# Spreading a pass's last projections, moving a residual product into the attention block and its loads with it

## The chip, the cores and the metric

One core of a Trainium2 chip runs the kernel. TensorE multiplies matrices, VectorE, ScalarE and GpSimd work elementwise, SyncE issues the loads and stores. The engines run on their own and wait for each other by semaphores. The metric is the device time of one execution, in microseconds.

## The reference

One layer of a perceiver, in f32. `x` is 512 x 512, the context 8192 x 512.

```python
x = x + cross_attention(layernorm(x), ctx)      # 16 heads of 32; q, k, v and output with bias bq, bk, bv, bo
x = x + sparse_self_attention(layernorm(x))     # per-head layernorm of q and k with an affine; sparse mixing
x = x + mixture_of_experts(layernorm(x))        # 8 experts, 2 per row
```

The change touches the first line and the layer norm that the second begins with:

```python
k = ctx @ Wk.T + bk; v = ctx @ Wv.T + bv
a = softmax(q @ k.T * 32 ** -0.5) @ v
x = x + a @ Wo.T + bo
h = (x - mean(x)) / sqrt(var(x) + 1e-5)
```

## The kernel before

The layer runs as a row of blocks. At the end of a block all engines meet before the next begins. A tensor of 512 x 512 is held as [128, 4, 512].

**First pass** (`prepare`, then `project_context`). The context comes in 16 chunks of 512 rows. Each chunk gives four outputs of 128 x 512 for the keys and four for the values, 128 outputs in all (`ITEMS` holds their order; the last three items are values). An output is the sum of 12 matmuls of 512 columns: `split_product` adds three products of high and low parts for each of four slices. Beside them run 256 steps of scores: step i writes scores of key differences (`dif`, one PSUM bank pair) and key sums (`tot`, two pairs); ScalarE takes the absolute value of `dif` (line 451), VectorE adds it to `tot` and keeps the maximum (line 480). On TensorE step i is: `scores(i + 1, dif)`, which waits until ScalarE has read the last `dif`; `scores(i, tot)`; and six projection matmuls, half an output, in steps 0 to 245. The last ten steps have none. In `finished(i)` ScalarE evacuates an output that is ready (`evacuate`: line 439 for keys, 443 for values), VectorE makes the low part of keys (`low`), and SyncE stores both to DRAM (line 340 for values). The block ends when the stores have landed.

**Second pass** (`attend_context`). Four groups of four heads; in each, 64 tiles of 128 context rows (16 chunks of four tiles). Per tile: scores of four heads (line 631), exponentials (ScalarE, line 694, two of 1024 columns), the weighted values (line 645), and on VectorE a running sum of the exponentials over runs of nine or ten tiles (lines 729 to 731), which `sums` adds up on TensorE (line 661). SyncE loads keys and values of chunk m into one of three buffers when chunk m - 3 has been scored (lines 599, 604). Behind chunk 2 it issues the output weights `woT`, the four weight matrices of self attention and the affine rows (lines 606, 861, 863). The shift of the next group's softmax is turned on TensorE in tile 9, copied by VectorE to `stage` (line 750), and taken by GpSimd into the rows of `c.stacks` (`take_row`, line 568); the scores of the next group wait for that. When a group is done, the sums are inverted (line 738) and `weigh` makes `aoT` from them: on GpSimd for the first three groups, on VectorE for the last (lines 572, 574).

**Residual** (`add_and_normalise` named "xo", a block of its own). For each of four tiles TensorE multiplies a row of ones by `bo` (line 790) and adds four products of `aoT` with `woT` (line 792; a product in f32 shows as two records), VectorE adds the tile to `x` and makes mean and variance (lines 805 to 811), ScalarE the square root, VectorE the inverse and the normalised tile (lines 814, 816). TensorE then turns all tiles (line 798), ScalarE and VectorE copy them to `hT`. Meanwhile SyncE loads the mixing weights (`load_mixing`): one part at once, the rest in 16 loads (line 854) when the last residual tile is done, since they overwrite `aoT` and `woT`.

**Self attention's projections** (`self_projections`). TensorE begins with queries (line 913). VectorE first waits for all mixing weights and reduces them (lines 986 to 995), and then centres the queries (line 958).

## Time and profile before

| | us |
|---|---|
| median of 3 runs | 1740.19 |
| the runs | 1730.46, 1740.19, 1740.70 |
| the profiled execution | 1736.88 |
| its span, first to last instruction | 1735.2 |
| TensorE (PE) busy in it | 1554.2, 90% |
| VectorE (DVE) busy | 1191.6, 69% |
| ScalarE (ACT) busy | 967.6, 56% |
| GpSimd (POOL) busy | 355.7, 20% |

The profile has these views: busy time by windows, with the clock that TensorE was granted (1.00 is 2.4 GHz, 0.50 is 1.2 GHz) and the busy share of the DMA engines; the timeline, in which neighbouring instructions of one kind are merged into a row with their count; and one line's or tile's instructions. PE is a matmul and PEld a weight load, SPq is SyncE's queue of DMAs. The end of a matmul is modelled, so its duration holds some of the pipeline; the distance between starts tells the rate. Rows of GpSimd are rough.

The first pass runs from 50 to 578 us, the second from 578.75 to 1171, the residual's block from there to 1201.5, self attention and the experts to the end.

### The profile page before, as it was taken

The page shows a single profiled execution, that of the slowest core. Times are in us where ns is not written, and L with a number is a line of the kernel's source. Part 1 is how long each engine was busy: PE and PEld are TensorE (multiplying, and loading weights), DVE is VectorE, ACT ScalarE, POOL GpSimd, SP SyncE. Part 2 cuts the span into 40 slices and gives each one's busy share as a digit, 9 for nine tenths or more (in the row PEclk, how much of TensorE's full clock was granted, in tenths as well). Part 3 has the DMA queues.
Part 4 walks back from the last instruction along what each step waited for, and adds up shares of the span by engine and source line. Part 5 has one row for each costly group of instructions (what it writes and reads, how often), then busy time and mean ns, then how long its engine had stood idle before and what let it go on. Part 6 is the DMA issues. An engine that isn't in the chain of part 4 may idle for free. (4 is left out here: it accounts for less than half of the span.)

```text
span 1735.2 us, 21727 instructions
## 1 busy us (share of the span) xinstructions
PE 1554.2 (90%) x8000; PEld 820.5 (47%) x8000; DVE 1191.6 (69%) x1836; ACT 967.6 (56%) x1165; POOL 355.7 (20%) x138
## 2 busy tenths in 40 slices
PE   6799999999999699999999999988877506699998
PEld 4466666666665233333333333323343204577775
DVE  5677677677676789999999999993865493220002
ACT  2466666666666678888888888860444501011110
POOL 4463563563560110030021001001000000100001
PEclk9899999999999699999999999998968857799999
DMA  4445445445345664444444444414100280379993
GB/s 171 175 164 184 142 161 185 142 159 188 136 162 146 197 143 121 116 115 118 115 120 122 121 116 118 117 40 73 31 19 1 85 309 2 111 246 327 326 329 109
DMA packets 117194, 250.00 MB, mean 144 GB/s; under 512 B 9689, under 2 KB 26073, under 8 KB 112610
## 3 DMA queue, kind: packets, MB, share of 16 engines
q1 hardware_dynamic: 115376, 244.42, 45.2%
q0 software_dynamic: 1280, 4.20, 0.7%
q8 instruction: 64, 1.05, 0.3%
q14 instruction: 40, 0.33, 0.1%
q10 hardware_dynamic: 434, 0.01, 0.0%
HBM read 182.00 MB, written 61.34 MB: 140 GB/s over the span
## 5 line engine op out<-in xcount | busy, mean ns | idle before, releaser
L694 ACT ACTIVATE att_pr<-att_sc 128x1024 f32<-128x1024 f32 x512 | 496.3, 1022 | 79.7 <-PE att_sc L631 79.7
L731 DVE TENSOR_TENSOR att_tot<-att_tot,att_pr 128x2048 f32<-128x2048 f32 x200 | 463.6, 2318 | 26.0 <-ACT att_pr L694 5.8
L480 DVE CUSTOM_DVE_ANT_0 ctx_size<-ctx_tot,ctx_size 128x512 f32<-128x512 f32 x512 | 332.9, 688 | 143.9 <-PE ctx_tot L399 139.8
L451 ACT ACTIVATE ctx_size<-ctx_dif 128x1024 f32<-128x1024 f32 x256 | 262.3, 1025 | 127.6 <-PE ctx_dif L399 127.6
L631 PE MATMUL att_sc<-g_stacks,att_kst 98*128 98x512 f32 x1024 | 309.9, 425 | 4.9 <-DMA att_kst<-keys_scratch 3.3
L631 PEld LDWEIGHTS att_sc<-g_stacks,att_kst 98*128 98x128 f32 x1024 | 173.9, 189 | 241.4 <-ACT att_pr L694 212.3
L645 PE MATMUL att_o<-att_pr,att_val 128*32 128x512 f32 x2048 | 274.5, 608 | 1.3 <-issue 1.2
L399 PE MATMUL ctx_dif<-ctx_k_dif,f_q_hi 32*128 32x512 f32 x512 | 129.4, 503 | 17.3 <-ACT ctx_size L451 10.1
L1661 ACT ACTIVATE ex_hidT<-ex_hp,m_b 128x128 f32<-128x128 f32 x120 | 34.2, 367 | 196.0 <-PE ex_hp L1616 193.6
L399 PE MATMUL ctx_tot<-ctx_k_sum,f_q_hi 32*128 32x512 f32 x512 | 130.0, 506 | 0.0
L1616 PEld LDWEIGHTS ex_hp<-ex_xT,m_w 128*128 128x128 f32 x960 | 109.4, 192 | 8.0 <-issue 8.0
L1616 PE MATMUL ex_hp<-ex_xT,m_w 128*128 128x128 f32 x960 | 109.8, 275 | 0.8 <-issue 0.8
L1629 PE MATMUL ex_yp<-m_w,ex_hidT 128*128 128x512 f32 x240 | 105.5, 592 | 0.0
L399 PEld LDWEIGHTS ctx_dif<-ctx_k_dif,f_q_hi 32*128 32x128 f32 x512 | 48.1, 184 | 112.7 <-issue 54.8
L101 POOL TENSOR_TENSOR g_stacks<-f_raw,g_stacks 128x2048 fp32r<-128x2048 f32 x21 | 96.7, 4604 | 1.7
L572 POOL TENSOR_TENSOR o_aoT<-att_whole,att_rs 128x512 f32<-128x512 f32 x3 | 9.4, 3138 | 385.6 <-DVE att_rs L738 385.6
L645 PEld LDWEIGHTS att_o<-att_pr,att_val 128*32 128x32 f32 x2048 | 40.5, 108 | 96.5 <-issue 95.2
L85 PE MATMUL f_proj<-g_stacks,f_wk_hi 128*128 128x512 f32 x176 | 78.0, 443 | 0.5 <-DVE f_k_lo L208 0.5
L1669 DVE COPY ex_xT<-ex_tx 128x512 f32<-128x512 f32 x15 | 10.4, 692 | 94.9 <-PE ex_tx L1570 88.8
L731 DVE TENSOR_TENSOR att_tot<-att_pr 128x2048 f32<-128x2048 f32 x28 | 64.0, 2287 | 14.1 <-ACT att_pr L694 14.1
L1675 DVE COPY o_yT<-ex_yp 128x512 f32<-128x512 f32 x15 | 10.4, 691 | 91.4 <-PE ex_yp L1629 91.4
L85 PE MATMUL f_proj<-f_wv_hi,g_stacks 128*128 128x512 f32 x160 | 71.3, 445 | 0.0
(273 smaller groups left out, 2118.6 us busy)
## 6 DMA issues: line engine op xcount, KB each, us to landing
m_w<-in_W SPq DMA_DIRECT2D x30, 2048.0 KB, 13.5
att_kst<-keys_scratch SPq DMA_DIRECT2D x192, 256.0 KB, 4.0
f_raw<-in_ctx SPq DMA_DIRECT2D x32, 1024.0 KB, 6.0
keys_scratch<-f_k_hi SPq DMA_DIRECT2D x32, 512.0 KB, 2.8
keys_scratch<-f_k_lo SPq DMA_DIRECT2D x32, 512.0 KB, 3.2
values_scratch<-ctx_v SPq DMA_DIRECT2D x32, 512.0 KB, 3.3
att_val<-values_scratch SPq DMA_DIRECT2D x64, 256.0 KB, 2.7
rows_scratch<-mix_blank SPq DMA_DIRECT2D x1, 3840.0 KB, 26.5
```

Source lines behind the costliest of these rows:

```text
L85: pe.matmul(out, ah, bh, start=(first and i == 0), stop=False)
L101: pool.tensor_tensor(c.lo[b], raw[:, :, :], f32(c.hi[b]), ALU.subtract).then_inc(c.s_lo, 1)
L399: mm = pe.matmul(out[:, r * CH:(r + 1) * CH], c.q_hi[rows, g, t * P:(t + 1) * P], keys[m % 2][rows, g, :], start=True, stop=True)
L451: act.activation(size[:, i % ABS, :], dif[:, :], ACT.Abs).then_inc(s_size, 1)
L480: dve.tensor_tensor_reduce(out=size[:, i % ABS, r * CH:(r + 1) * CH], in0=tot[i % 2][:, r * CH:(r + 1) * CH], in1=size[:, i % ABS, r * CH: ...
L631: mm = pe.matmul(sc[pair % PAIRS][:, r * N:(r + 1) * N], kst[m % CHUNKS][:, j, at:at + P], c.stacks[0:STK + 2, HG * (T // PER_G) + j, :], ...
L645: mm = pe.matmul(o[at, :], val[m % CHUNKS][:, T % KT, at], pr[:, T % SLOTS, j, :], start=first, stop=False, skip_group_check=True)
L694: act.activation(pr[:, T % SLOTS, 2 * s:2 * s + 2, :], sc[(2 * T + s) % PAIRS][:, :].rearrange("p (j q) -> p j q", j=2), ACT.Exp, scale=SC ...
L731: dve.tensor_tensor(tot[b % 2][:, :, :], so_far, pr[:, T % SLOTS, :, :], ALU.add).then_inc(s_add, 1)
L1616: mm = pe.matmul(hp[tau % 2][:, f, :], w1[b][:, k, f * P:(f + 1) * P], xT[tau % 2][:, k, :], start=(k == 0), stop=(k == DC - 1))
L1629: mm = pe.matmul(yp[tau % 2][:, :], hidT[tau % 2][:, f, :], w2[b][:, f, :], start=(f == 0), stop=(f == FC - 1))
L1661: act.activation(hidT[tau % 2][:, f, :], hp[tau % 2][:, f, :], ACT.Relu, bias=b1[:, f, :]).then_inc(s_hid, 1)
```

## The change

`split_product` takes a range of the 12 matmuls of an output. The first 228 steps of the first pass have six of them as before, steps 228 to 254 have four. The block "xo" is gone. The bias comes broadcast over 128 partitions and is added to `x` by GpSimd early in the second pass. In the second pass's own block TensorE multiplies the three finished groups with the output weights, for tile 0 before the last sums and for tiles 1 to 3 after them, then adds the last group; VectorE normalises tile t - 1 after the moments of tile t, tiles are turned one by one, and ScalarE alone copies them. The affine rows are loaded after chunk 8, self attention's matrices after chunks 17, 19, 21 and 23, the output weights after chunk 32; the mixing weights are loaded in this block too. The core of the diff:

```diff
@@ project_context
-    LAST = 2 * (len(ITEMS) * KT - FIRST)
+    WHOLE = 3 * DC
+    WIDE, NARROW = WHOLE // 2, WHOLE // 3
+    CUT = (WHOLE * (len(ITEMS) * KT - FIRST) - NARROW * (STEPS - 1)) // (WIDE - NARROW)
+    def begun(i):
+        return WIDE * min(i, CUT) + NARROW * max(i - CUT, 0)
+    def pieces(i):
+        at, end = begun(i), min(begun(i + 1), WHOLE * (len(ITEMS) * KT - FIRST))
+        while at < end:
+            stop = min(end, at - at % WHOLE + WHOLE)
+            yield FIRST + at // WHOLE, at % WHOLE, at % WHOLE + stop - at
+            at = stop
     def finished(i):
-        return [FIRST + (i - 1) // 2] if i % 2 == 0 and 0 < i <= LAST else []
+        return [o for o, _, end in pieces(i - 1) if end == WHOLE] if i else []
...
                 scores(i, tot[i % 2], k_sum, s_tot)
-                if i < LAST:
-                    project(FIRST + i // 2, i % 2)
+                for piece in pieces(i):
+                    project(*piece)
@@ attend_context
+        xh = pr[:, (TILES - 2) % SLOTS - 2, :, :]
+        banks = [sc[(2 * TILES - n) % PAIRS][:, half * N:(half + 1) * N] for n in (3, 2, 1) for half in range(2)]
+        acc, tp = banks[0:NT], banks[NT:] + [o[:, :], den[:, :]]
@@ gpsimd, after the memsets
+            pool.wait_ge(s_ones, CHUNKS)
+            pool.wait_ge(bo_in, 16)
+            for t in range(NT):
+                pool.tensor_tensor(c.x[:, t, :], c.x[:, t, :], c.yT[:, 2, :], ALU.add).then_inc(s_bo, 1)
+            pool.wait_ge(s_bo, NT)
@@ sync, in the loop over chunks m
-                if m == CHUNKS - 1:
+                if m == NCH // 2:
+                    sp.dma_start(c.yT[:, 2, :], c.dram["bo"].broadcast_to([P, D])).then_inc(bo_in, 16)
+                    load_affine(sp, c)
+                if NCH <= m < NCH + 2 * len(SELF_WEIGHTS) and m % 2:
+                    load_self_weight(sp, c, m // 2 - NCH // 2)
+                if m == 2 * NCH:
                     sp.dma_start(c.woT[:, :, :], ...).then_inc(c.wo_in, 16)
-                    load_self_weights(sp, c)
+            sp.wait_ge(s_row[0], HG // 2 + HG * (G - 1))
+            sp.wait_ge(s_bo, NT)
+            load_mixing(sp, c, s_mm)
@@ tensor, after the last tile
+            pe.wait_ge(c.wo_in, 16)
+            pe.wait_ge(s_out, G - 1)
+            residual(0, range(G - 1))
             sums(len(starts) - 1)
+            for t in range(1, NT):
+                residual(t, range(G - 1))
+            pe.wait_ge(s_out, G)
+            for t in range(NT):
+                residual(t, [G - 1]).then_inc(s_mm, 1)
+            for t in range(NT):
+                pe.wait_ge(s_h, t + 1)
+                for k in range(DC):
+                    mm = pe.transpose(tp[t][:, k * P:(k + 1) * P], xh[:, t, k * P:(k + 1) * P], c.ident[:, :])
+                mm.then_inc(s_tp, 1)
@@ scalar, after the last exponential
+            for t in range(NT):
+                act.wait_ge(s_var, t + 1)
+                act.activation(std[:, t:t + 1], std[:, t:t + 1], ACT.Sqrt).then_inc(s_std, 1)
+                if t >= 1:
+                    turned_rows(t - 1)
+            turned_rows(NT - 1)
@@ vector, after weigh(dve, G - 1)
+            dve.wait_ge(s_bo, NT)
+            for t in range(NT):
+                moments(t)
+                if t >= 1:
+                    normalised(t - 1)
+            normalised(NT - 1)
@@ perceiver_layer
                 attend_context(nc, c)
-                add_and_normalise(nc, c, "xo", c.aoT, c.woT, c.wo_in, c.hT, bias=c.bo[:, :],
-                                  meanwhile=load_mixing)
```

`residual(t, groups)` multiplies `aoT` with `woT` for those groups into `acc[t]`; `moments(t)` is the addition, the two statistics and the epsilon of the old block, `normalised(t)` its inverse and product; `turned_rows(t)` copies one turned tile.

## Rows read from the trace of the kernel before

**Rows 1.** Windows by stage: window, us, busy us (instructions) by engine, granted clock, DMA share, GB/s.

```profile
564.40:574.00 9.60, 4.02 (x24) 1.48 (x24) 6.60 (x21) 5.12 (x5) 0.00 (x0) 0.50 0.00 0
...
621.20:722.00 100.80, 100.80 (x589) 38.82 (x588) 92.25 (x41) 88.02 (x91) 0.00 (x0) 1.00 0.47 118
...
1201.50:1206.00 4.50, 4.46 (x7) 1.92 (x8) 0.00 (x0) 0.00 (x0) 4.21 (x2) 0.62 1.06 140
```

**Rows 2.** Timeline, first pass, a step with six projection matmuls: start us, us, engine, line, operation.

```profile
553.42 0.50 PE L399 MATMUL ctx_dif<-ctx_k_dif,f_q_hi 32*128 32x512 f32 x2
...
554.20 0.40 PE L86 MATMUL f_proj<-f_wv_lo,f_third 128*128 128x512 f32 x1
...
554.43 0.40 PE L87 MATMUL f_proj<-f_wv_hi,f_third 128*128 128x512 f32 x1
...
555.46 0.49 PE L399 MATMUL ctx_dif<-ctx_k_dif,f_q_hi 32*128 32x512 f32 x2
...
555.56 0.60 ACT L443 ACTIVATE ctx_v<-f_proj 128x512 f32<-128x512 f32 x1 [0.57 <-PE f_proj L87]
```

**Rows 3.** Timeline, first pass, steps without projections, and the next block's first load.

```profile
561.19 0.50 PE L399 MATMUL ctx_dif<-ctx_k_dif,f_q_hi 32*128 32x512 f32 x2 [1.16 <-ACT ctx_size L451]
...
562.80 0.50 PE L399 MATMUL ctx_dif<-ctx_k_dif,f_q_hi 32*128 32x512 f32 x2 [1.11 <-ACT ctx_size L451]
...
573.98 0.79 PE L399 MATMUL ctx_dif<-ctx_k_dif,f_q_hi 32*128 32x512 f32 x2 [1.11 <-ACT ctx_size L451]
...
578.75 1.28 SPq L599 DMA_DIRECT2D att_kst<-keys_scratch  x3
```

**Rows 4.** Line 340, the stores of values in the first pass.

```profile
DMA to landing us min/median/max: 3.0/3.3/4.2
```

**Rows 5.** Timeline, SyncE's queue in the second pass: the fourth chunk's keys.

```profile
601.11 1.37 SPq L599 DMA_DIRECT2D att_kst<-keys_scratch  x3
```

**Rows 6.** Timeline, second pass, around the wait for keys.

```profile
609.27 1.94 ACT L694 ACTIVATE att_pr<-att_sc 128x1024 f32<-128x1024 f32 x2 [0.19 <-PE att_sc L631]
...
615.08 1.06 PE L631 MATMUL att_sc<-g_stacks,att_kst 98*128 98x512 f32 x2 [3.33 <-DMA att_kst<-keys_scratch]
...
619.04 1.94 ACT L694 ACTIVATE att_pr<-att_sc 128x1024 f32<-128x1024 f32 x2 [1.76 <-PE att_sc L631]
...
621.17 1.94 ACT L694 ACTIVATE att_pr<-att_sc 128x1024 f32<-128x1024 f32 x2 [0.19 <-PE att_sc L631]
```

**Rows 7.** Line 731 from 750 to 766 us (ns min/median/max), and GpSimd's timeline beside it.

```profile
L731 DVE TENSOR_TENSOR att_tot<-att_tot,att_pr x5: 2227/2294/3179, 747.8 to 761.2; 128x2048 f32<-128x2048 f32 x5
...
755.86 3.14 POOL L572 TENSOR_TENSOR o_aoT<-att_whole,att_rs 128x512 f32<-128x512 f32 x1 [138.07 <-DVE att_rs L738]
```

**Rows 8.** Timeline, from the last sums to self attention's first products.

```profile
1165.47 1.06 PE L661 MATMUL att_den<-att_tot,g_ones 128*32 128x512 f32 x8 [2.28 <-DVE att_tot L731]
...
1190.11 3.70 PE L792 MATMUL xo_acc<-a_woT,o_aoT 128*128 128x512 f32 x8
...
1193.85 0.69 DVE L805 TENSOR_TENSOR g_x<-xo_acc,g_x 128x512 f32<-128x512 f32 x1 [2.86 <-PE xo_acc L792]
...
1195.59 0.15 DVE L814 RECIPROCAL xo_rstd<-xo_std 128x1 f32<-128x1 f32 x1
...
1197.43 3.67 SPq L854 DMA_DIRECT2D a_woT<-in_spOT  x8
...
1197.55 0.15 DVE L814 RECIPROCAL xo_rstd<-xo_std 128x1 f32<-128x1 f32 x1
...
1199.04 1.08 ACT L830 ACTIVATE g_hT<-xo_tp 128x512 f32<-128x512 f32 x2 [3.13 <-PE xo_tp L798]
...
1201.54 15.67 PE L913 MATMUL sp_queries<-a_swqT,g_hT 128*128 128x512 f32 x32 [2.54 <-PEq L768]
...
1211.05 2.29 DVE L986 TENSOR_REDUCE sp_vm<-o_yT 128x16 f32<-128x2048 f32 x1 [10.72 <-DMA a_woT<-in_spOT]
...
1218.64 2.29 DVE L958 TENSOR_REDUCE sp_total<-sp_queries 128x64 f32<-128x2048 f32 x1
```

More of the change, by code:

```diff
@@ L76, in allocators, with split_product @@
     return sb, pb, sem
-def split_product(pe, out, a, b, last=True, first=True):
-    n = len(a)
-    for i in range(n):
-        (ah, al), (bh, bl) = a[i], b[i]
-        pe.matmul(out, ah, bh, start=(first and i == 0), stop=False)
-        pe.matmul(out, ah, bl, start=False, stop=False)
-        mm = pe.matmul(out, al, bh, start=False, stop=(last and i == n - 1))
+def split_product(pe, out, a, b, begin=0, end=None):
+    end = 3 * len(a) if end is None else end
+    for n in range(begin, end):
+        (ah, al), (bh, bl) = a[n // 3], b[n // 3]
+        left, right = ((ah, bh), (ah, bl), (al, bh))[n % 3]
+        mm = pe.matmul(out, left, right, start=(n == 0), stop=(n == 3 * len(a) - 1))
     return mm
@@ L172, in _ @@
         def _(act):
-            for name, tile in (("bq", c.bq), ("bk", c.bk), ("bv", c.bv), ("bo", c.bo)):
+            for name, tile in (("bq", c.bq), ("bk", c.bk), ("bv", c.bv)):
                 act.dma_start(tile[:, :], c.dram[name]).then_inc(small_in, 16)
@@ L370, in _, with project @@
         def _(pe):
-            def project(o, part):
+            def project(o, begin, end):
                 kind, n = ITEMS[o // 4]
                 b, at, out = o // 4 % RING, o % 4, proj[o % 2][:, :]
-                if part == 0:
+                if begin == 0:
                     if at == 0:
@@ L381, in project @@
                         pe.wait_ge(v_done, count("v", o - 1))
-                ks = range(DC // 2 * part, DC // 2 * part + DC // 2)
+                ks = range(DC)
                 cols = slice(at * P, at * P + P)
@@ L389, in project @@
                     second = [(c.wv_hi[:, k, :], c.wv_lo[:, k, :]) for k in ks]
-                mm = split_product(pe, out, first, second, first=(part == 0), last=(part == 1))
-                if part == 1:
+                mm = split_product(pe, out, first, second, begin, end)
+                if end == WHOLE:
                     mm.then_inc(s_out, 1)
@@ L679, in _, with residual @@
                     turn(pe, den)
-            sums(len(starts) - 1)
+            def residual(t, groups):
+                for g in groups:
+                    mm = pe.matmul(acc[t], c.aoT[:, g, t * P:(t + 1) * P], c.woT[:, g, :],
+                                   start=(g == 0), stop=(g == G - 1))
+                return mm
+            pe.wait_ge(c.wo_in, 16)
+            pe.wait_ge(s_out, G - 1)
+            residual(0, range(G - 1))
+            sums(len(starts) - 1)
+            for t in range(1, NT):
[8 more added lines that the diff above has]
+                mm.then_inc(s_tp, 1)
         @block.scalar
@@ L761, in _, with moments, normalised, add_and_normalise @@
             weigh(dve, G - 1)
[L762 to L766 removed]
+            def moments(t):
+                dve.wait_ge(s_mm, t + 1)
+                dve.tensor_tensor(c.x[:, t, :], acc[t], c.x[:, t, :], ALU.add).then_inc(s_x, 1)
+                dve.wait_ge(s_x, t + 1)
+                dve.bn_stats(stats[:, t, :], c.x[:, t, :]).then_inc(s_stats, 1)
+                dve.wait_ge(s_stats, 2 * t + 1)
+                dve.bn_aggr(mv[:, t, :], stats[:, t, :]).then_inc(s_stats, 1)
+                dve.wait_ge(s_stats, 2 * t + 2)
+                dve.tensor_scalar(std[:, t:t + 1], mv[:, t, 1:2], EPS, None, ALU.add).then_inc(s_var, 1)
+            def normalised(t):
+                dve.wait_ge(s_std, t + 1)
+                dve.reciprocal(rstd[:, t:t + 1], std[:, t:t + 1]).then_inc(s_rstd, 1)
+                dve.wait_ge(s_rstd, t + 1)
+                dve.tensor_scalar(xh[:, t, :], c.x[:, t, :], mv[:, t, 0:1], rstd[:, t:t + 1],
+                                  ALU.subtract, ALU.mult).then_inc(s_h, 1)
+            dve.wait_ge(s_bo, NT)
[4 more added lines that the diff above has]
+            normalised(NT - 1)
+            dve.wait_ge(s_h, NT)
+def add_and_normalise(nc, c, name, srcT, w, w_in, hT, h):
     with ExitStack() as stack:
@@ L780, in add_and_normalise @@
         block = stack.enter_context(nc.Block())
-        if meanwhile is not None:
-            meanwhile(nc, c, block, s_mm)
         @block.tensor
@@ L788, in _ @@
             for t in range(NT):
-                if bias is not None:
-                    pe.matmul(acc[t][:, :], c.one_row[:, :], bias, start=True, stop=False)
                 for k in range(DC):
                     mm = pe.matmul(acc[t][:, :], srcT[:, k, t * P:(t + 1) * P], w[:, k, :],
-                                   start=(bias is None and k == 0), stop=(k == DC - 1))
+                                   start=(k == 0), stop=(k == DC - 1))
                 mm.then_inc(s_mm, 1)
```

56 lines of the change are left out of this document (30 added, 26 removed).

## The prediction

> **What bounds the kernel now.** I read the windows by stage first, then the timeline around the three places that the change touches, then the SyncE queue and the waits there. In the second pass TensorE is the bound: busy 100.80 of 100.80 us in the first group of heads, with VectorE next at 92.25 and ScalarE at 88.02 [rows 1]. An engine that is full in one stage says nothing of the seams between the stages, and all parts of the change lie at seams: the end of the first pass, the start of the second, and what stands between the second pass and self attention.
>
> End of the first pass. While a step carries six projection matmuls, TensorE sets its pace: steps start 2.04 us apart (553.42, 555.46), with projection matmuls 0.23 apart [rows 2]. Without projections the pace is a loop: the scores `dif`, ScalarE's absolute value, and only then the next `dif`, since that has one bank: 1.61 us at the full clock [rows 3]. In the last steps TensorE is busy 4.02 of 9.60 us and its granted clock is 0.50, the lower of its two levels (1.2 instead of 2.4 GHz) [rows 1]. The reader is to see a stretch in which TensorE is over its limit, then one in which it idles.
>
> Start of the second pass. TensorE waits 3.33 us at 615.08 for a load of keys [rows 6]. That load, of the fourth chunk, was issued at 601.11 [rows 5], since SyncE had the output weights, four matrices of self attention and the affine rows to issue before it, 5 MB in all. It took 14 us to arrive.
>
> End of the second pass. TensorE has nothing from the last weighted product to 1165.47, then the sums, then again nothing while VectorE inverts and weighs; the residual product, its normalisation and the turns follow as a block of their own, until self attention's first matmul at 1201.54 [rows 8].
>
> **Part A, four matmuls per step.** 123 outputs of 12 matmuls are 1476. Now steps 0 to 227 have six and 228 to 254 have four: 228 x 6 + 27 x 4 = 1476. Nothing is removed; it is spread. Cost of a step: 2.04 less two matmuls of 0.23 is 1.58 us on TensorE, just below the loop's 1.61; I take 1.62. ScalarE's evacuation (0.60 us, now every third step) starts 0.10 after the next `dif` [rows 2] and fits in the 0.59 that ScalarE would otherwise wait (1.61 less the absolute value's 1.02, 5.12 us for five [rows 1]); without that cover it costs up to 0.6 x 9 = 5.4 us. The last nine outputs are values, so VectorE has no low part to make.
>
> Before: 553.42 is step 243, so step 228 began at 553.42 - 15 x 2.03 = 522.97 (2.03 a step: from 553.42 to 561.19 there are three of them and one of 1.68, the first without projections but with an evacuation), and the last `dif` at 573.98 came 51.0 us later [rows 2, 3]. After: 26 x 1.62 = 42.1. Gain 8.9 us, some 2 of it because the clock stays up. What is late next: the last values are evacuated only now. For six matmuls the evacuation began 2.14 us after its step's start (555.56 - 553.42), for four 1.68; with 0.60 for itself, 3.3 for the store to land [rows 4] and 0.5 for the change of block, the next block starts 6.1 us after the last `dif` instead of 4.77 (578.75 - 573.98) [rows 3]. That gives back 1.3. A = 7.5 us; bounds 3.5 (steps of 1.75, store 4.2) and 8.9.
>
> **Part B, loads.** SyncE no longer issues the five matrices before chunk 3. Between ScalarE's exponentials at 609.27 and 621.17 lie six of 1024 columns, so three tiles; a tile takes 2.13 (619.04 to 621.17) [rows 6], in all 6.4, and 0.4 for four transposes of 128 columns (an estimate, a quarter of a matmul record's 0.43 each): 11.9 - 6.8 = 5.1 us won, bounds 3.3 (the wait alone) and 5.3. TensorE sets that stage, so nothing else takes it. The loads now stand one by one: bias and affine rows after chunk 8, a matrix after each of chunks 17, 19, 21 and 23, the output weights after 32. Each is followed in SyncE's queue by the keys of the next chunk, which are issued two chunks, 8 tiles x 2.13 = 17 us, before they are used. 5 MB delayed a load to 14 us; 1 MB leaves over 10 us of slack. Cost nothing.
>
> GpSimd now waits for the bias and adds it to four tiles of x before it takes the rows of the second group. Chunk 8 is issued when chunk 5 is scored, near 640 us; four additions at 3.14 (the nearest row) [rows 7] and the rows end before 675. They are needed when the second group's scores begin, near 730. Hidden by over 50 us; without that cover it would cost what it is late by. Beside one such GpSimd addition a VectorE addition took 3.18 instead of 2.29 us [rows 7]. Four may cost VectorE 3.6 us, at most 12.6. It has 8.5 us free in this stretch [rows 1] and may lag six tiles: nothing.
>
> The Trainium skill (SBUF — State Buffer, Who interferes with whom) says that a VectorE instruction with two SBUF inputs and a GpSimd one that reads SBUF lock each other out, wholly, by order of issue. By that rule VectorE could stand for 4 x 3.14 = 12.6 us; the lengthened row agrees in kind and shows less.
>
> **Part C, residual.** TensorE is free 2.28 us before 1165.47 [rows 8]. Tile 0 with the three finished groups takes 6 records (a product in f32 is two) 0.43 apart, 2.6 us, so the sums start 0.3 late, at 1165.8. VectorE's reciprocal, product and bias end 5.7 us after the sums' start: 1171.5. Meanwhile TensorE does 18 records for the other tiles, 7.7 us behind sums of 1.06: until 1174.6. So TensorE, not the weighing, decides. The last group: first tile done at 1174.6 + 0.86 + 0.3 = 1175.7. The four matmuls with a row of ones are gone, and the clock no longer falls first.
>
> VectorE: add, statistics, aggregate and epsilon are 1.74 per tile (1193.85 to 1195.59), normalising 0.65 (1.96 for three, 1195.59 to 1197.55): 4 x 1.74 + 4 x 0.65 = 9.6, until 1185.3. It overlaps the other residual tiles, which it could not before, being paced by them. From the last normalisation to ScalarE's copy 0.84 (1198.20 to 1199.04), copy 0.6, change of block 0.5: 1187.2 for the first matmul of self attention. SyncE's sixteen loads, 7.3 us of issue from the last residual on (1193.85 to 1201.10), now end at 1185.7 and no longer hold the block back. Gain 14.3. One block fewer is in this; Sqrt's table loads behind the last exponential.
>
> Next: VectorE reduces the mixing weights when they have landed, 17.2 us after the last residual matmul (1193.85 to 1211.05), and needs 7.6 us, to 1218.64. Now 1178.3 + 17.2 + 7.6 = 1203.1; the queries end at 1187.2 + 15.7 = 1202.9. VectorE goes on at 1203.1, 15.5 us earlier. For 4.5 us the queries ran at a mean clock of 0.62 [rows 1]; the idle stretch before them is now longer, so I take off 0.5: C = 15.0. Bounds: 12 (clock low through the turns and 7 us of queries, 0.3 more for each step of the chain) and 16.
>
> **Sum.** 7.5 + 5.1 + 15.0 = 27.6 us. The profiled execution took 1736.88 us (span 1735.2): 1709.3. The three runs have their median at 1740.19, two at 1740 and one at 1730, so the profiled one lies in the middle of them; by the median it would be 1712.6. I take 1711.
>
> **Rivals.**
> 1. The evacuation is not covered, or steps are paced otherwise: A falls to 3.5, time 1715. For it: 1.58 and 1.61 are close. Against: the six-matmul steps show no delay of the absolute value over 0.1 us. Chance 0.12.
> 2. The shorter seam leaves TensorE at the low clock: C 12, time 1714. Chance 0.12.
> 3. The port lock between GpSimd and VectorE is not absorbed: 12.6 - 8.5 = 4.1 us, time 1715. By the skill's page (same section) the lock is total. Chance 0.04.
> 4. The other side: the loads, one by one, stall TensorE each as the block of five did. Place: behind chunks 8, 17, 19, 21, 23, 32. Price 5.1 each, 30.6 us: 1714, or 1741 with all six. It makes the kernel slower from the sixth stall on, or from 4.6 us per stall without part B, and only if a 1 MB load delays keys beyond their 17 us. Chance 0.03, nearly all at one or two stalls.
> 5. It doesn't do what it says: the seam after the first pass is set by something not seen, such as the new values' store, and A is nothing; 1718. Chance 0.04.
>
> Forecast 0.65. The range 1701 to 1721 goes down to the upper bounds (8.9 + 5.3 + 16 = 30.2, from the fastest run 1700.3) and up to the lower (3.5 + 3.3 + 12 = 18.8, from the median 1721.4).
>
> About 1% (17 us) can be told from no change here, since the three runs alone spread over 0.6%. Faster by over 1% means a gain over 17.4, just below my lower bound: 0.87. Within 1%: 0.11. Slower: 0.02.
>
> **What would show it.** Steps of 1.61 to 1.65 us from about 523 on, clock 1.00 up to 567, `dif` last at about 565; first load of the next block about 571; no wait for keys near 605; exponentials 2.13 apart throughout; VectorE additions lengthened near 635 only; from sums to first self matmul 22 us instead of 36. Wrong if steps exceed 1.75, if TensorE waits for keys between 700 and 860, or if the queries begin later than 22 us after the sums.

## The result, and the profile after

| us | before | changed |
|---|---|---|
| median of the runs | 1739.81 (4 runs, 1730.46 to 1740.70) | 1711.64 (4 runs, 1709.72 to 1716.72) |
| the profiled execution | 1736.88 | 1716.72 |
| its span | 1735.2 | 1715.0 |

The ratio is 0.9846, with a 95% interval of 0.9804 to 0.9887. Two later comparisons of the same program with the kernel before gave 0.9875 [0.9855, 0.9896] and 0.9856 [0.9824, 0.9889]. The kernel is faster by 23 to 28 us in the three comparisons; 1711.0 us was predicted and 1711.64 measured.

Where the time went, read from the first and last rows of each stretch in both timelines:

| stretch | before | changed | gain |
|---|---|---|---|
| start to step 228 of the first pass | 522.98 | 523.90 | -0.9 |
| step 228 to the last `dif` | 51.00 | 42.21 | 8.8 |
| last `dif` to the second pass's first load | 4.77 | 5.82 | -1.1 |
| first load to the last exponential | 582.3 | 577.8 | 4.5 |
| last exponential to self attention's first matmul | 40.5 | 26.9 | 13.6 |
| from there until self attention clears its `shift` rows (VectorE, line 1177 before, 1265 changed) | 64.0 | 64.8 | -0.7 |
| from there to the end | 469.6 | 473.6 | -4.0 |
| sum | 1735.2 | 1715.0 | 20.2 |

Five of the stretches are the change's: 8.8 - 1.1 + 4.5 + 13.6 - 0.7 = 25.1 us. The first and the last run code that it doesn't touch. The first differs by more between two executions of one program: step 228 starts at 518.76 to 525.30 us in three profiles of the changed kernel. Of the 4.0 us in the last, 1.5 come back in every profile of the changed kernel. They stand at self attention's residual product, some 170 us after the shift (first row before, second changed):

```profile
1436.24 13.97 PE L792 MATMUL so_acc<-o_swoT,o_yT 128*128 128x512 f32 x32 [1.59 <-PEq L1212]
1414.62 15.52 PE L877 MATMUL so_acc<-o_swoT,o_yT 128*128 128x512 f32 x32 [1.59 <-PEq L1300]
```

The first four microseconds of this product run at a granted clock of 1.00 before and 0.61 changed. It takes 13.97 us in all four profiles of kernels with the old block "xo" and 15.46 to 15.52 in eight profiles with the new seam. In two kernels that differ from the changed one only at the seam before the queries, `late` and `warm_tail`, it is 13.97 again. So it hangs on what the kernel does at that seam, over 230 us earlier; why is open. The rest of the 4.0 is not shown to be the change's.

End of the first pass, from the timeline of the changed kernel (start us, us, engine, line, operation; ACT L462 is the absolute value, L454 the evacuation, SPq is SyncE's queue):

```profile
527.20 0.50 PE L411 MATMUL ctx_dif<-ctx_k_dif,f_q_hi 32*128 32x512 f32 x2
527.74 1.03 ACT L462 ACTIVATE ctx_size<-ctx_dif 128x1024 f32<-128x1024 f32 x1 [0.59 <-PE ctx_dif L411]
528.82 0.50 PE L411 MATMUL ctx_dif<-ctx_k_dif,f_q_hi 32*128 32x512 f32 x2
528.87 0.60 ACT L454 ACTIVATE ctx_v<-f_proj 128x512 f32<-128x512 f32 x1
529.36 1.03 ACT L462 ACTIVATE ctx_size<-ctx_dif 128x1024 f32<-128x1024 f32 x1
...
566.11 0.50 PE L411 MATMUL ctx_dif<-ctx_k_dif,f_q_hi 32*128 32x512 f32 x2
...
567.78 0.60 ACT L454 ACTIVATE ctx_v<-f_proj 128x512 f32<-128x512 f32 x1
568.40 0.36 SPq L352 DMA_DIRECT2D values_scratch<-ctx_v  x1
...
571.93 1.28 SPq L625 DMA_DIRECT2D att_kst<-keys_scratch  x3
```

The steps are 1.62 apart (527.20, 528.82). The absolute value of 527.74 follows an idle 0.59 of ScalarE, that of 529.36 has none in front: the evacuation between them took exactly that gap and moved nothing. The windows (busy us and instructions of PE, PEld, DVE, ACT, POOL, then the granted clock, DMA share, GB/s) show a TensorE that is full at 1.00, where before it idled at 0.50 [rows 1]:

```profile
524.00:566.10 42.10, 42.04 (x208) 22.36 (x208) 33.69 (x103) 31.18 (x35) 0.00 (x0) 1.00 0.49 126
...
613.60:714.40 100.80, 100.80 (x590) 38.89 (x592) 96.41 (x41) 88.15 (x91) 22.77 (x8) 1.00 0.47 123
```

Start of the second pass, same view; around the fourth chunk's keys, where TensorE had waited 3.33 [rows 6], there is no gap over 0.57 between the exponentials. The self attention matrices are issued later, one by one, in 0.43 to 0.44 each:

```profile
587.66 1.25 SPq L625 DMA_DIRECT2D att_kst<-keys_scratch  x3
...
605.07 1.94 ACT L748 ACTIVATE att_pr<-att_sc 128x1024 f32<-128x1024 f32 x2 [0.57 <-PE att_sc L665]
...
715.38 0.43 SPq L945 DMA_DIRECT2D a_swqT<-in_sWqT  x1
```

The first row is the keys of the fourth chunk, asked for at 587.66, 15.7 us after the block's first load; before it was 22.4 (601.11 less 578.75) [rows 3, 5]. TensorE's waits from 625 to 1148 us, the view by what was waited for, hold no DMA at all:

```profile
engine line waited for: us in total, times, longest us
PE att_o L679 <- issue: 1.9, 3, 1.0
```

GpSimd's additions of the bias and its casts of the rows, and VectorE's long additions beside both (the second view gives ns, minimum, median, maximum):

```profile
638.88 12.55 POOL L604 TENSOR_TENSOR g_x<-g_x,o_yT 128x512 f32<-128x512 f32 x4 [61.58 <-DMA o_yT<-in_bo]
651.50 10.41 POOL L589 CAST g_stacks<-o_yT 2x512 fp32r<-2x512 f32 x4
```

```profile
L798 DVE TENSOR_TENSOR att_tot<-att_tot,att_pr x10: 2292/2512/3206, 635.7 to 664.2; 128x2048 f32<-128x2048 f32 x10
L798 DVE TENSOR_TENSOR att_tot<-att_pr x1: 3373/3373/3373, 646.9 to 646.9; 128x2048 f32<-128x2048 f32 x1
```

End of the second pass, which answers to [rows 8]. L717 is the residual product, L695 the sums, L832 VectorE's addition to `x`, L844 the normalised tile, L733 the turns, L754 their copies, L936 the sixteen mixing loads, L1001 the queries, L1074 the reduction of the mixing weights, L1046 the centring:

```profile
1149.70 1.03 ACT L748 ACTIVATE att_pr<-att_sc 128x1024 f32<-128x1024 f32 x1 [0.19 <-PE att_sc L665]
1150.75 1.28 ACT L759 ACT_TABLE_LOAD   x1
1151.78 2.84 PE L717 MATMUL att_sc<-a_woT,o_aoT 128*128 128x512 f32 x6
1154.55 1.06 PE L695 MATMUL att_den<-att_tot,g_ones 128*32 128x512 f32 x8
1155.55 11.43 PE L717 MATMUL att_sc<-a_woT,o_aoT 128*128 128x512 f32 x26
1159.80 0.49 DVE L595 TENSOR_SCALAR o_aoT<-o_aoT,g_bv 128x512 f32<-128x512 f32 x1
1164.50 0.69 DVE L832 TENSOR_TENSOR g_x<-att_sc,g_x 128x512 f32<-128x512 f32 x1 [4.22 <-PE att_sc L717]
...
1170.59 3.66 SPq L936 DMA_DIRECT2D a_woT<-in_spOT  x8
...
1173.59 0.55 DVE L844 TENSOR_SCALAR att_pr<-g_x,att_mv,att_rstd 128x512 f32<-128x512 f32 x1
1174.45 1.06 PE L733 MATMUL att_den<-g_ident,att_pr 128*128 128x128 f32 x4
...
1175.54 0.60 ACT L754 ACTIVATE g_hT<-att_den 128x512 f32<-128x512 f32 x1 [0.26 <-PE att_den L733]
1176.62 16.76 PE L1001 MATMUL sp_queries<-a_swqT,g_hT 128*128 128x512 f32 x32 [1.11 <-PEq L542]
...
1184.82 2.29 DVE L1074 TENSOR_REDUCE sp_vm<-o_yT 128x16 f32<-128x2048 f32 x1 [10.68 <-DMA a_woT<-in_spOT]
...
1193.42 2.29 DVE L1046 TENSOR_REDUCE sp_total<-sp_queries 128x64 f32<-128x2048 f32 x1 [1.03 <-PE sp_queries L1001]
```

From the sums to the first matmul of self attention it is 22.07 us, where it was 36.07. The weighing is done at 1160.29 under TensorE's 26 records, which run on without a gap; VectorE then waits 4.22 for the first tile; the table load hides behind the last weighted product. The queries take 16.76 instead of 15.67, and the windows say why:

```profile
1167.00:1176.60 9.60, 3.28 (x16) 2.42 (x17) 6.72 (x19) 3.00 (x7) 0.00 (x0) 0.76 0.98 137
1176.60:1182.00 5.40, 5.38 (x7) 2.30 (x8) 0.00 (x0) 0.00 (x0) 5.12 (x2) 0.50 0.99 126
```

While the tiles are normalised and turned one by one, TensorE works 3.28 of 9.60 us, its clock falls, and the queries' first 5.4 us run at 1.2 GHz.

### The profile page after: what moved, and what is told of

It is laid out like the page before. It is cut to its first block and busy times, and to the rows that moved or that the text cites. A ratio compares the mean times of both kernels' runs of the same rounds, so it can differ in the third digit from the quotient of the medians.

```text
span 1715.0 us, 21707 instructions
## 1 busy us (share of the span) xinstructions
PE 1551.6 (90%) x7992; PEld 820.3 (48%) x7992; DVE 1195.3 (70%) x1834; ACT 969.8 (57%) x1167; POOL 374.4 (22%) x141
## 5 line engine op out<-in xcount | busy, mean ns | idle before, releaser
L462 ACT ACTIVATE ctx_size<-ctx_dif 128x1024 f32<-128x1024 f32 x256 | 262.4, 1025 | 123.6 <-PE ctx_dif L411 123.6
L1749 ACT ACTIVATE ex_hidT<-ex_hp,m_b 128x128 f32<-128x128 f32 x120 | 34.4, 368 | 195.9 <-PE ex_hp L1704 195.9
L86 PE MATMUL f_proj<-f_wv_hi,g_stacks 128*128 128x512 f32 x320 | 120.7, 420 | 0.0
L86 PE MATMUL f_proj<-g_stacks,f_wk_hi 128*128 128x512 f32 x352 | 119.5, 421 | 0.8 <-DVE f_k_lo L206 0.8
L86 PEld LDWEIGHTS f_proj<-g_stacks,f_wk_hi 128*128 128x128 f32 x352 | 60.3, 189 | 29.7 <-issue 20.1
```

The source lines that it names most:

```text
L86: mm = pe.matmul(out, left, right, start=(n == 0), stop=(n == 3 * len(a) - 1))
L462: act.activation(size[:, i % ABS, :], dif[:, :], ACT.Abs).then_inc(s_size, 1)
L1749: act.activation(hidT[tau % 2][:, f, :], hp[tau % 2][:, f, :], ACT.Relu, bias=b1[:, f, :]).then_inc(s_hid, 1)
```

## The experiments

Twelve runs were made, two of them of the changed kernel again, in three sessions with their own runs of the kernel before (medians 1742.12, 1742.93 and 1740.67 us; the first two sessions on one chip, the third on another). Single executions of one program differ by several us, so the stretches are compared as well as the times.

### Part A alone, and the clock

`a_only` is the kernel before with the new `split_product` and `project_context`. `clock_only` and `clock_kept` leave the projections as they were and fill the last steps of the kernel before:

```diff
                 if i < LAST:
                     project(FIRST + i // 2, i % 2)
+                elif LAST + 1 < i < STEPS - 1:           # clock_kept: i < STEPS - 1
+                    if i == LAST + 2:                    # clock_kept: i == LAST
+                        pe.wait_ge(v_done, count("v", 4 * len(ITEMS) - 1))
+                    for _ in range(4):
+                        pe.matmul(proj[0][:, :], c.wv_hi[:, 0, 0:P], c.wv_hi[:, 1, :], start=True, stop=True)
```

> The kernel before with the new step plan alone (six matmuls in steps 0 to 227, four in 228 to 254). Theory: the parts are separate and add up; the first pass, from the start of step 228 to the next block's first load, takes 48.0 us instead of 55.8, and the kernel is 7.7 us faster, ratio 0.9955. Rival: the gain of this part is partly eaten later, since the keys' loads and the clock of the second pass depend on it: under 5 us.

> The kernel before with four matmuls more in each of steps 248 to 254, whose sums nobody reads; the projections stay where they were. It parts the clock from the spreading. Theory: the steps at the end are a loop of scores, absolute value, scores; at the full clock it is 1.61 us instead of 1.91, so the last eight steps give 2.1 to 2.4 us and no more, and the other 6.5 us of part A come from matmuls that moved out of steps of 2.03. Rival: the steps without projections are 1.91 for another reason than the clock, and nothing changes; or four matmuls lengthen the loop beyond 1.61.

> The kernel before, with four further matmuls of 512 columns in each of the steps 246 to 254, right behind the last projection, so that TensorE never idles before them; their result is used nowhere. Theory (1.5 us of part A is the clock): the granted clock stays 1.00 to the last dif and the last eight intervals between dif's starts are 1.62 each, 13.0 us, instead of 1.68, 1.61, 1.62 and five of 1.91, 14.5 in all; the first pass is 1.5 us shorter and nothing else changes. Rival (four matmuls fill a step at any clock and cost as much as they give): intervals of 1.8 and more, no gain.

`a_only`: step 228 to the last `dif` 42.19 us (before 51.00), last `dif` to the next block 5.84, so 7.7 us in the stage; 1735.73 us, ratio 0.9965 [0.9948, 0.9981], 6.4 us. The sum and its sign hold, so rival 5 is out.

`clock_only`: 1743.06 us, ratio 1.0011 [0.9987, 1.0035]. It did not do what it was made for. TensorE had already idled for two steps, the clock fell as the first of the added matmuls ran, and they were then too long for a step:

```profile
565.67 1.50 PE L428 MATMUL f_proj<-f_wv_hi 128*128 128x512 f32 x4
567.10 0.79 PE L399 MATMUL ctx_dif<-ctx_k_dif,f_q_hi 32*128 32x512 f32 x2
567.83 2.07 PE L428 MATMUL f_proj<-f_wv_hi 128*128 128x512 f32 x4
```

Two steps of 1.86 and 2.73 (565.24 to 567.10 to 569.83) cost what the later steps at full clock gave back. `clock_kept`, with no idle step in between, is the clean test. The windows of its last steps, with the clock, and of the same stretch of the kernel before:

```profile
561.60:574.70 13.10, 13.05 (x69) 6.94 (x68) 10.14 (x33) 8.71 (x9) 0.00 (x0) 1.00 0.12 41
```

```profile
561.20:574.00 12.80, 5.02 (x32) 1.85 (x32) 9.12 (x29) 7.16 (x7) 0.00 (x0) 0.61 0.12 40
```

Its last eight intervals between starts of `dif` are 1.67, then 1.62 to 1.63: 13.03 us, against 14.47 before. So 1.4 us of part A is the clock, where the prediction said "some 2", and the other 7.4 of its 8.8 are work moved into free time. Its time of 1738.35 is a single run and says nothing finer.

`clock_kept` shows one thing more, for part B. Its second pass is that of the kernel before, the loads in the old place, and yet TensorE does not wait for keys. The waits from 590 to 640 us, in the kernel before:

```profile
engine line waited for: us in total, times, longest us
PE att_sc L631 <- DMA att_kst<-keys_scratch: 3.3, 1, 3.3
```

In `clock_kept` the same view is empty. The last of the fourth chunk's three key loads landed 31.6 us after the block's first load, against 35.7 to 36.3 in the four other profiles with the loads in the old place (`before`, `clock_only`, `a_only`, `b_back`), which wait 3.3, 2.8, 4.0 and 2.6 us. First to last exponential takes 569.5 us, no longer than the 570.3 of the changed kernel on the same chip.

### Why four matmuls, and not three

```diff
-    WIDE, NARROW = WHOLE // 2, WHOLE // 3
+    WIDE, NARROW = WHOLE // 2, WHOLE // 4
```

> The changed kernel with three projection matmuls in each of the last 18 steps (237 to 254) instead of four in each of the last 27. Theory (a cheap step is paced by the loop of dif and ScalarE's absolute value, so a third fewer matmuls don't shorten it): the 18 steps stay at 1.62, the nine steps that are full again cost 0.41 more each, and from step 228 to the last dif it takes 9 x 2.03 + 17 x 1.62 = 45.8 us instead of 42.2, 3.7 us longer. Rival (TensorE's matmuls set a cheap step): 1.62 - 0.23 = 1.39 us a step, 9 x 2.03 + 17 x 1.39 = 41.9, no longer than now. The clock is expected to stay at 1.00; should it fall, the steps show 1.9.

Measured (one run, 1720.41 us): the cheap steps stay at 1.62, now eighteen of them, and from what was step 228 to the last `dif` it takes 45.80 us, as the theory had it, 3.6 more than with four. The timeline shows who sets such a step:

```profile
560.43 0.50 PE L411 MATMUL ctx_dif<-ctx_k_dif,f_q_hi 32*128 32x512 f32 x2 [0.21 <-ACT ctx_size L462]
...
562.05 0.50 PE L411 MATMUL ctx_dif<-ctx_k_dif,f_q_hi 32*128 32x512 f32 x2 [0.22 <-ACT ctx_size L462]
```

With three matmuls TensorE waits 0.21 to 0.22 in a step for the absolute value; with four, one more matmul of 0.23 fills that and the wait is gone from the rows. Four is where both are full.

### Part B taken back

```diff
-                if NCH <= m < NCH + 2 * len(SELF_WEIGHTS) and m % 2:
-                    load_self_weight(sp, c, m // 2 - NCH // 2)
-                if m == 2 * NCH:
+                if m == CHUNKS - 1:
                     sp.dma_start(c.woT[:, :, :], ...).then_inc(c.wo_in, 16)
+                    for n in range(len(SELF_WEIGHTS)):
+                        load_self_weight(sp, c, n)
```

> The changed kernel with the five matrices issued in one go behind chunk 2 again; bias and affine rows stay behind chunk 8. Theory: the wait for the keys of chunk 3 comes back, about 3.3 us on TensorE and 4.5 to 5.1 us on the end: about 1716 us where the changed kernel has 1711.6. Rival: the wait was owed to the affine rows and to the order at the block's start, and the time stays.

Measured: 1722.57 us, ratio 0.9895 [0.9863, 0.9926]. The wait is back, at the fourth chunk's keys:

```profile
589.30 3.85 SPq L625 DMA_DIRECT2D att_kst<-keys_scratch  x3
...
607.29 0.73 PE L665 MATMUL att_sc<-g_stacks,att_kst 98*128 98x512 f32 x2 [2.62 <-DMA att_kst<-keys_scratch]
...
609.41 2.08 PE L665 MATMUL att_sc<-g_stacks,att_kst 98*128 98x512 f32 x4
```

SyncE needs 3.85 us instead of 1.25 to issue the three loads behind the 5 MB, and the last of them lands 14 us after that. From the first to the last exponential it takes 574.6 us instead of 570.1 to 570.3 in three profiles of the changed kernel: B is 4.4 us in this profile. It is nothing in an execution that has no wait, as that of `clock_kept`; how often that is, five profiles can't say. The times put 2.5 us between `b_back` and the changed kernel in a later session on the same chip (1722.57 and 1720.11), and their intervals overlap. Of this 2.62 is the wait for keys; half a tile later the scores run 2.08 for four instead of 1.20, and two exponentials come 1.50 and 0.73 late.

### Part C: the early product against the lost block

```diff
-            residual(0, range(G - 1))
             sums(len(starts) - 1)
-            for t in range(1, NT):
-                residual(t, range(G - 1))
             pe.wait_ge(s_out, G)
             for t in range(NT):
-                residual(t, [G - 1]).then_inc(s_mm, 1)
+                residual(t, range(G)).then_inc(s_mm, 1)
```

> The changed kernel, but the whole residual product stands behind the last group's weighing, still inside the block. It parts the early product from the lost block and bias. Theory: TensorE waits 4.7 us for the weighing, its clock falls, the first residual tile is done after 3.4 us at the full clock or 6.8 at the half, and VectorE is then paced by tiles: self attention's first matmul comes 3 to 7 us later than in the changed kernel, about 30 to 34 us after the last exponential instead of 26.9. Rival: VectorE's 9.6 us decide alone, and it is under 1 us later.

Measured: 1726.76 us, ratio 0.9912 [0.9881, 0.9943]; from the last exponential to the queries 34.4 us instead of 26.9.

```profile
1157.85 15.48 PE L717 MATMUL att_sc<-a_woT,o_aoT 128*128 128x512 f32 x32 [4.72 <-DVE o_aoT L595]
...
1176.95 3.67 SPq L933 DMA_DIRECT2D a_woT<-in_spOT  x8
```

```profile
1151.20:1157.90 6.70, 1.98 (x9) 0.25 (x9) 4.99 (x4) 0.00 (x0) 0.00 (x0) 0.50 0.00 0
```

TensorE stands 4.72 us for the weighing, at the low clock, and then paces VectorE tile by tile, 3.4 apart. The last load is issued at 1180.62, and the queries start 0.44 later: SyncE's sixteen issues end this block, as they ended the old one (1201.10 to 1201.54). So of the 13.6 us 7.5 come from computing the product early. The other 6.1 are left for the lost block, the bias outside and the normalisation that overlaps; no run parts these three.

### Trying to gain more at the seams

`early_vm` computes the last tile's four groups in one go, so that the last groups of tiles 0 to 2 come before it, and lets the reduction of the value-mixing weights wait for those loads alone:

```diff
-            for t in range(1, NT):
+            for t in range(1, NT - 1):
                 residual(t, range(G - 1))
             pe.wait_ge(s_out, G)
-            for t in range(NT):
+            for t in range(NT - 1):
                 residual(t, [G - 1]).then_inc(s_mm, 1)
+            residual(NT - 1, range(G)).then_inc(s_mm, 1)
...
-            dve.wait_ge(c.mix_in, 16 * 5 * HG)
+            dve.wait_ge(c.mixv_in, 16 * HG)
```

> The changed kernel with another order of the residual product: tiles 1 and 2 with the three finished groups, then the last group for tiles 0 to 2, then tile 3 whole; and the values' part of the mixing weights, which landed long before, has a semaphore of its own and is reduced while the rest is on its way. Theory: VectorE gets tile 0 at 7.4 us after the last sums instead of 9.95, self attention's first matmul comes 1.9 to 2.6 us earlier (SyncE's issues may hold the block: the bound is then 1.9), and the centring of the queries too. Rival: the last mixing loads land at the same time, so the centring gains under 1 us; without the early reduction it would be 1.0.

Measured: 1717.97 us, ratio 0.9849 [0.9826, 0.9873], beside 1720.11, 0.9875 [0.9855, 0.9896], of the changed kernel on the same chip (`after_again`). The intervals overlap, so the times show no gain; the stage does. VectorE has tile 0 7.4 us after the sums instead of 9.95, the queries start 25.0 us after the last exponential instead of 26.9, and their centring comes 2.1 earlier. The early reduction gave nothing that can be seen: the centring waits for TensorE's queries with it and without.

> The changed kernel once more, as the measure for the others of this chip and for what differs between two executions of one program. Theory: from the last exponential to self attention's first matmul 26.9 us again, and from the first exponential to the last 570 us; what comes after the centring of the queries differs by some us from one execution to the next, as the spans before (516.6 us) and after (521.6 us) did where nothing was changed. Rival: the 5.0 us after the centring belong to the change, and show again in full.

`after_again` has 26.9 and 570.1 us again. From the queries' centring to the end it takes 524.9, where the first profile had 521.6 and the kernel before 516.5. Without the experts, whose length changes from execution to execution (last section), it is 280.7 to 281.1 in three profiles of the changed kernel and 276.1, 278.0, 278.0 and 279.2 in four with the old block. So the rival holds for about half of its 5.0 us: 1.0 up to self attention's shift and 1.5 at its residual product are the change's.

`warm_tail` keeps TensorE busy between the turns, `warm_head` before the second pass's first scores; the results of the added instructions are used nowhere:

```diff
@@ after the turns of tile t (warm_tail: t < NT - 1; best2: t < NT - 2)
+                    for _ in range(2):
+                        pe.matmul(acc[0], c.ident[:, :], val[0].rearrange("p k d -> p (k d)"), start=True, stop=True)
@@ before the second pass's first turn (warm_head), and five more behind it
+            for _ in range(16):
+                pe.transpose(den[:, 0:P], c.ident[:, :], c.ident[:, :])
```

> The changed kernel with two f32 matmuls of 512 columns, whose sums nobody reads, after the turns of each of the tiles 0 to 2: work for TensorE while VectorE normalises. Theory: the clock stays at its upper level through the turns and at the start of the queries, whose 32 matmuls then take 14 us instead of 16.8, and the last two turns 0.66 instead of 1.1: the centring of the queries 2.5 to 3 us earlier. Rival: the level at the start of the queries does not hang on the 7 us before them, and the queries take 15.7 to 16.8.

> The changed kernel with 16 turns of a constant before the first turn of the second pass and five behind it, in time in which TensorE waits for VectorE, ScalarE and GpSimd. Theory: the scores of the first tiles run at the upper clock level, the sixth exponential does not wait 1.34 us, and the first tiles save 1.2 to 2 us. Rival: the start is set by the loads of values and the exponentials, and nothing is saved.

`warm_tail` (one run, 1718.23): the turns and the queries run at 1.00.

```profile
1170.90:1179.60 8.70, 7.56 (x28) 3.71 (x28) 5.10 (x14) 2.79 (x6) 0.00 (x0) 1.00 1.04 129
1179.60:1185.00 5.40, 5.36 (x13) 2.52 (x14) 0.00 (x0) 0.00 (x0) 5.10 (x2) 1.00 1.06 132
```

```profile
1179.64 13.97 PE L1004 MATMUL sp_queries<-a_swqT,g_hT 128*128 128x512 f32 x32 [1.11 <-PEq L542]
```

The queries take 13.97 instead of 16.76; they start 0.85 later, since the added matmuls hold up the last turn. The low clock in that place costs 2.8 us, and with it gone self attention's residual product is back at 13.97 us too. `warm_head` (one run, 1717.39): the first exponential comes 6.92 after the block's first load instead of 7.59, and first to last takes 568.6 instead of 570.2: 2.3 us for the two.

`best2` joins the three, with added matmuls behind tiles 0 and 1 only; `after_ref` is the changed kernel beside it.

> The changed kernel with four edits: a run of turns of the unit matrix by itself before the second pass's first scores; the last residual tile's four groups in one go, so that tile 0 reaches VectorE sooner; the reduction of the value-mixing weights waits for those loads alone; and two unused matmuls behind the turns of tiles 0 and 1, to keep TensorE busy before the queries (three tiles had them before, and the last turn came 0.8 us late for it). If the gains seen singly add up: 2.2 at the head of the second pass, 2.2 from the reordering, 1 to 2 from the warmer tail: 5 to 6 us less than the changed kernel, ratio to before about 0.984 where the changed kernel has 0.987. Rival: the reordering and the warmer tail end at the same wait (VectorE's reductions, then the queries), so only one of them counts: 3 to 4 us.

> The changed kernel unaltered, beside the others on the same chip. Ratio to before 0.985 to 0.988. It also gives a third profile of one program: if the pitch of the six-matmul steps (2.023 and 2.007 in the two so far) and the length of the experts' stage (240.4 or 244.2) belong to the execution and not to the program, they show some value of 2.007 to 2.037 and one of those two levels again.

Measured: `best2` 1714.75 us (6 runs), 0.9844 [0.9813, 0.9875]; `after_ref` 1717.12 (6 runs), 0.9856 [0.9824, 0.9889]. The intervals overlap: a gain of 2.4 us isn't shown by the times. The stages, from the second pass's first load to self attention's shift, say 664.7 us against 669.5, 4.9 less: 1.9 at the head, 3.0 behind the last exponential. That is just below the 5 to 6 of the theory and above the rival's 3 to 4. The queries again run in part at the low clock (15.67 us); that the third turn, left without cover, is the reason is argued and not tested.

## Why the prediction was right, point by point

**Part A, 7.5 predicted, 7.7 measured.** Steps of 1.62, 42.2 us instead of 42.1, the clock at 1.00, the evacuation free: each term as worked out. What is late next was named rightly, the last values' store, and sized 0.3 too high (5.8 from the last `dif` instead of 6.1). That all 27 steps fit rested on two numbers close together, 1.58 and 1.61; the three-matmul run puts them about 0.01 us apart (a wait of 0.22, a matmul of 0.23). The share of the clock was 1.4 us, not 2.

**Part B, 5.1 predicted, 4.4 to 4.5 measured.** Mechanism and place are right: the fourth chunk's keys. The wait alone (3.33) was too little and the count of tiles from exponential to exponential too much. What the prediction did not see is that the wait is no fixed property of the kernel before: one profile in five with the loads in the old place has none, and there B would give nothing. Rival 4 did not happen: no wait for a DMA in the rest of the pass. Its arithmetic is off: one stall of 5.1 makes 1716 and not 1714, and without part B (22.5 us left) the kernel becomes slower from 3.8 us per stall, not from 4.6, which is 27.6 / 6.

**The four additions.** They took 12.55 us and ended at 651.4, well before 675. With the rows, which took 10.41, GpSimd was done at 661.9. VectorE's four additions beside GpSimd's took 3.19, 3.21, 3.37 and 3.19 us instead of 2.29, 3.8 more in all, where 3.6 was taken and 12.6 was the bound. The four beside the casts took 2.51, 0.9 more in all; the busy 96.41 us of the window, against 92.25 [rows 1], hold both. VectorE absorbed it: from 636 to 675 us the exponentials of the tiles stay 2.13 apart but for the steps of 2.98 that come with the sums every 20 us. The Trainium skill (SBUF — State Buffer, Who interferes with whom) has the lock whole. The prediction made 12.6 us of that from GpSimd's recorded durations, and VectorE lost 3.8. This does not show that the lock is partial: a recorded 3.3 us of GpSimd can hold its own waiting for VectorE. For it: the first of the four additions took 1.93 to 2.73 us in five profiles and not 3.3, as it found VectorE's addition partly done, and a cast takes 2.56 beside VectorE's additions and 0.61 beside none. What VectorE loses is then GpSimd's own share of the time, some 0.9 us an addition. No run has a GpSimd addition without VectorE beside it, so this stays a reading.

**Part C, 15.0 predicted, 12.9 measured.** The chain up to the last normalised tile is right almost row by row: the sums 0.4 late (0.3 predicted), tile 0 at VectorE 9.95 after the sums (9.9), VectorE's chain 9.6 (9.6), SyncE's loads no longer at the end. Then two terms fail.

First, 0.84 us was taken from the last normalisation to the copy, from a row of before; it is 1.40 (1174.14 to 1175.54), since the last turns run at the low clock, 1.06 instead of 0.66. With that the queries start 13.6 earlier, not 14.3.

Second, the step "VectorE goes on at 1203.1, 15.5 us earlier" took the queries' centring as what counts. It did come 13.9 us earlier (17.1 us after the queries' start before, 16.8 now), yet what follows it, up to self attention's shift, became 1.0 longer. The next meeting of the two engines is the centring of the keys. It needs VectorE to be done with the queries, 12.46 us after it begins on them, and TensorE to be done with the keys, which it multiplies right behind the queries. Times are us after the queries' first matmul:

| kernel | queries' 32 records | queries' centring | keys' centring | shift | what came last before the keys' centring |
|---|---|---|---|---|---|
| `warm_tail` | 13.97 | 15.2 | 27.7 | 62.0 | both, within 0.03 |
| before | 15.67 | 17.1 | 29.6 | 64.0 | VectorE |
| `clock_only` | 15.67 | 17.7 | 30.2 | 64.6 | VectorE |
| `a_only` | 15.67 | 17.9 | 30.4 | 64.9 | VectorE |
| `best2` | 15.67 | 15.7 | 29.4 | 63.7 | TensorE |
| `early_vm` | 16.39 | 16.4 | 30.2 | 64.4 | TensorE |
| changed | 16.76 | 16.8 | 30.5 | 64.8 | TensorE |

The rows before and changed, where the second has a wait and the first has none:

```profile
1231.10 2.28 DVE L958 TENSOR_REDUCE sp_total<-sp_keys 128x64 f32<-128x2048 f32 x1
1207.15 2.29 DVE L1046 TENSOR_REDUCE sp_total<-sp_keys 128x64 f32<-128x2048 f32 x1 [1.20 <-PE sp_keys L1001]
```

With the old block VectorE is the path: with queries of the same length, 15.67, the shift comes later by what the centring comes later, 0.8 us for 0.8. But it is so by little: in the kernel before the keys were done 0.16 us before their centring. In the changed kernel the slow queries push the end of the keys from 29.4 to 30.5, TensorE becomes the path, and VectorE waits 1.20. So the prediction's chain through VectorE's reductions was the right one for the kernel before, and what it missed is that the keys' matmuls stand right behind it: bringing the centring forward is worth nothing beyond them, and the low clock costs its full 1.1 us there. Against the queries' start the keys' centring comes 1.0 later, of which 0.2 are back by the shift, so the gain of C is the 13.6 of the queries' start less 0.7. The 1.5 us at self attention's residual product are in no term of the prediction; with them C is 11.4.

**The rivals.** Rivals 1, 3, 4 and 5 did not occur. Rival 2, the low clock at the seam, occurred in good part: C is 12.9, nearer to that rival's 12 than to the forecast's 15. The prediction knew that the clock would fall there and took off 0.5; the runs say 2.8 for the queries against a full clock, of which the kernel before already paid 1.7, so that 1.1 was to be taken off, and the 1.5 further on.

**The sum.** 27.6 us was forecast and the five stretches give 25.1: A 7.7, B 4.5, C 12.9. With the 1.5 us further on it is 23.6. That the median came out within 1 us of 1711.0 is partly luck: the two later comparisons have 22.8 and 23.6 us instead of 28.2, and their medians for the changed kernel are 1720.1 and 1717.1. The range of 1701 to 1721 was about right for what executions do.

## What to carry to other kernels

At a seam between two stages look for what each engine does not do there: work with an early operand (three of four groups of a product) can be done under a wait that can't be shortened, and it keeps the clock up besides. When work is spread into steps that are paced by a loop of other engines, fill them exactly to the loop: four matmuls were free, six were not, and three threw 3.6 us away. Follow a gain down to where the engines meet next and ask which comes second there, and by how little: VectorE was the path to the keys' centring by some 0.1 us, so most of what the prediction hoped to gain on it beyond the queries' start could not be had. And look for a wait in several executions before you price its removal.

## What the runs showed of the hardware

**One program, several paces.** With six matmuls a step of the first pass takes 2.023, 2.007 and 2.023 us in three profiles of the changed kernel (the 64 steps from 65 to 129 in 129.49, 128.42 and 129.49 us), and 2.007 to 2.037 over the profiles of all kernels. The code of these steps, their order and the granted clock of 1.00 are the same. Over 228 steps, 0.016 us are 3.6 us. The experts, from their first matmul to the end of the run, take 240.3 to 241.0 us in five profiles and 243.9 to 244.7 in nine, and the changed kernel shows both (240.5, 244.2, 243.9). Why is open; but a difference of a few us between two single profiles means nothing until the stretch is named.

**The clock falls late, under work.** In `clock_only` TensorE idled most of two steps from 562 on, and it was granted full speed in them; the matmuls that ended the idling then ran slow, at 0.83 in the mean of the next 9.8 us:

```profile
561.00:566.50 5.50, 3.23 (x20) 1.74 (x19) 4.13 (x13) 3.76 (x5) 0.00 (x0) 0.99 0.27 95
566.50:576.30 9.80, 9.80 (x42) 4.91 (x40) 6.88 (x23) 5.43 (x6) 0.00 (x0) 0.83 0.00 0
```

Filling a gap after it has begun can cost as much as it gives; filled from its first step (`clock_kept`), the clock never moved. And what happens at one seam shows at a later one: self attention's residual product starts at 1.00 or at 0.61 by what the seam before the queries was like, 230 us earlier.

**Two engines slow each other.** It shows on both sides. VectorE's additions of 2.29 us take 3.19 to 3.37 beside GpSimd's additions and 2.51 beside its casts. GpSimd's four casts take 2.56 each beside VectorE's additions; in the kernel before, where VectorE had nothing to do from 615.3 us to 620.1, the last three took 0.61 each.
